# The first turn of two wide attentions: when the late tiles' statistics are taken, and the order of cycle 1's work on three engines

## The chip, the cores and the metric

The kernel runs on one core of a Trainium2 chip. The metric is the device time in microseconds; lower is better.

## The reference

The whole program is eight stages on x (8 batches of 256 tokens by 128) with a context of 8 x 512 x 96. Before each stage x is normalised over its 128 features, and each stage's result is added to x. Two of the stages, the third and the fourth cross attention, are the wide attentions that the change touches. Cut to what matters, with 8 heads of 64 in the one and 16 heads of 64 in the other:

```python
z = layernorm(x)
q, k, v = z @ Wq, ctx @ Wk, ctx @ Wv            # split in heads of 64
sim  = einsum('bihd,bjhd->bhij', q, k) * 64 ** -0.5
attn = softmax(sim)
x = x + einsum('bhij,bjhd->bihd', attn, v).reshape(...) @ Wo + bo
```

## The kernel before, in words

`wide_attention` (line 1945) builds both stages: `l2_attention` (names l2a, 8 heads) and `l3_attention` (names l3a, 16 heads). A **turn** is one of the 8 batches, a **cycle** (c) one pair of heads, so a turn has 4 cycles in l2a and 8 in l3a. In a cycle there are 4 units u: two tiles of 128 queries for two heads, each 128 x 512 scores. Turn 0 is written out by itself (`is_first`), the others run in a loop. Nothing is planned at run time: each engine has its instructions in the order in which the functions below write them, and waits on semaphores.

The way of one cycle: TensorE makes the scores (line 2095) in two halves; VectorE takes the negated maximum of each half (`maxima`, line 2337); ScalarE takes the exponentials of the four units with their sums (`exps`, line 2251); VectorE inverts two sums at a time (`invert`, line 2343); GpSimd multiplies the probabilities by them (line 2039); TensorE turns the four units over (`turned`, line 2108), and VectorE copies units 0 and 2 (`keep_turned`, line 2349), ScalarE units 1 and 3 (line 2258) out of PSUM. This turning over is done one cycle later than the scores, and `weighted` (line 2119: probabilities by values) two cycles later; VectorE's `keep_o` (line 2354) takes its result out of the bank `work[0]`. Queries and keys for the cycle two ahead are projected in between (`project_q` lines 2055 to 2057, `project_k` lines 2068 to 2070, `project_v` lines 2081 to 2083); ScalarE keeps the high part (`keep_q` line 2234, `keep_k` line 2240, `keep_v` line 2244), VectorE the low part (`q_low` line 2327, `k_low` line 2332).

The waits that bear on the change: `turned` of unit 2 waits until VectorE has copied unit 0 out of the same bank, and that of unit 3 for ScalarE's copy of unit 1. `project_v` waits for the `k_low` before it. `weighted` waits for the next `q_low`, and `project_q` for `keep_o`, since they share a bank. `project_k` waits for the `keep_v` before it.

**The late tiles.** Four tiles of 128 tokens are normalised only inside turn 0 of each wide attention, by a class `Ahead` (line 305): `statistics` on VectorE (line 334 four times, line 338 four times, and line 340, which adds epsilon to the variance), the power -1/2 on GpSimd (`gpsimd`, line 345), `apply` on VectorE (line 350 four times) at the end of cycle 2, the turning over on TensorE (line 370) in cycle 3, and its high and low part by ScalarE and VectorE (`keep` line 375, `low` line 379). TensorE turns over cycle 2's unit 0 only when `low` is done (`late.z_lo_ready`). Before the change `statistics` stands in cycle 2 behind both `maxima` and ahead of `keep_o`, and the power between units 1 and 2 of cycle 2 on GpSimd.

Of the kernel before, what the change touches and what calls it, by code (L numbers as in the profile page):

```python
# [1944 lines left out]
def wide_attention(nc, g, name, HEADS, wq, wk, wv, wo, bo, last_tiles, last_tokens, norm_all):  # L1945
# [9 lines left out]
    with ExitStack() as scope:  # L1955
# [16 lines left out]
        ahead = Ahead(s, g, TPB)  # L1972
        late = Ahead(s, g, len(last_tiles), "late")
        late_x = [g.x[:, i, :] for i in last_tiles]
# [20 lines left out]
        def is_first(b):  # L1995
            return isinstance(b, int) and b == 0
# [18 lines left out]
        @block.gpsimd  # L2015
        def _(e):
            def split_ctx(b, side):
                high, low = c_hi[side % SIDES], c_lo[side % SIDES]
                wait(e, m.c_lo_ready, b)
                e.tensor_copy(cT[:, :], g.ctxT[0:DC, bass.ds(b * S, S)]).then_inc(m.c_taken, 1)  # L2020
                e.wait_ge(m.c_taken, b)
                wait(e, m.k_projected, C * (b + 1 - SIDES))
                e.tensor_tensor(high[:, :], cT[:, :], bcast(g.ones[0:DC, 0:1], [DC, S]), ALU.mult).then_inc(m.c_hi_ready, 1)
                e.wait_ge(m.c_hi_ready, b + 1)
                e.tensor_tensor(low[:, :], cT[:, :], high[:, :], ALU.subtract).then_inc(m.c_lo_ready, 1)

            def turn(b, side, more):
                xs = g.x[:, bass.ds(TPB * b, TPB), :]
                e.tensor_tensor(xs, xs, bcast(bo[:, :].unsqueeze(1), [P, TPB, D]), ALU.add).then_inc(m.x_biased, 1)
                for c in range(C):  # L2030
                    for u in range(UNITS):
                        if u == 2 and c == 2:
                            late.gpsimd(e, 0) if is_first(b) else ahead.gpsimd(e, b - 1)
                        if u == 2 and c == C - 3 and more and SIDES == 1:
                            split_ctx(b + 1, 1 - side)
                        if u % 2 == 0:
                            e.wait_ge(m.rinv_ready, 2 * (C * b + c) + u // 2 + 1)
                        n = slot(c, u)
                        e.tensor_tensor(prob[n][:, :], prob[n][:, :], bcast(rinv[:, n:n + 1], [P, S]),  # L2039
                                        ALU.mult).then_inc(m.prob_ready, 1)  # L2040
                    if c == C - 4 and more and SIDES == 2:
                        split_ctx(b + 1, 1 - side)

            turns(e, turn)
            if norm_all:
                ahead.gpsimd(e, B - 1)
# [181 lines left out]
        @block.scalar  # L2228
        def _(e):
            def keep_q(b, c):  # L2230
                n = C * b + c
                e.wait_ge(m.q_projected, n + 1)
                wait(e, m.scores_ready, 2 * (n - 1))
                e.activation(q_hi[c % 2][:, :], work[0][:, 0:T], ACT.Copy, scale=SCALE).then_inc(m.q_hi_ready, 1)

            def keep_k(b, c):
                n = C * b + c
                e.wait_ge(m.k_projected, n + 1)
                wait(e, m.scores_ready, 2 * (n - 1))
                e.activation(k_hi[c % 2][:, :], work[1][:, :], ACT.Copy).then_inc(m.k_hi_ready, 1)  # L2240

            def keep_v(b, c, side, src=work[1]):
                e.wait_ge(m.v_projected, C * b + c + 1)
                e.activation(values_of(side)[:, c % KT, c // KT * 512:(c // KT + 1) * 512], src[:, :], ACT.Copy).then_inc(m.v_kept, 1)

            def exps(b, c, u):
                n, at = C * b + c, slot(c, u)
                if u % 2 == 0:
                    e.wait_ge(m.max_ready, 2 * n + u // 2 + 1)
                wait(e, m.turned, UNITS * (n - 2) + u + 1)  # L2250
                e.activation(prob[at][:, :], bank(u), ACT.Exp, bias=nmax[:, at:at + 1],  # L2251
                             accum_out=rsum[:, at:at + 1]).then_inc(m.exp_ready, 1)

            def keep_turned(b, c, u):
                n = C * b + c
                e.wait_ge(m.turned, UNITS * n + u + 1)
                wait(e, m.o_ready, n - 1)
                e.activation(pT[c % 2][:, :, u % 2, u // 2 * P:u // 2 * P + P],  # L2258
                             tps[u % 2][:, :].rearrange("p (t q) -> p t q", q=P), ACT.Copy).then_inc(m.pT_kept_act, 1)

            def keep_z(b):
                ahead.keep(e, b, g.zT[:, bass.ds(b * T, T)], tps[0][:, 0:T])

            def turn(b, side, more):
                first = is_first(b)
                for c in range(C):
                    onward = c + AHEAD < C or more
                    on = (b, c + AHEAD, side) if c + AHEAD < C else (b + 1, c + AHEAD - C, 1 - side)
                    turn_c = (b, c - 1) if c >= 1 else (b - 1, C - 1)
                    turns_here = c >= 1 or not first  # L2270
                    if c == 0 and first:
                        keep_q(0, 1)
                        exps(b, c, 0)
                        keep_k(0, 1)
                        exps(b, c, 1)
                        exps(b, c, 2)
                        keep_v(0, 0, 0, tps[0])
                        exps(b, c, 3)
                        keep_v(0, 1, 0, tps[1])
                        continue  # L2280
                    if c == 1 and first:
                        keep_v(0, 2, 0)
                        exps(b, c, 0)
                        keep_q(0, 2)
                        exps(b, c, 1)
                        keep_turned(0, 0, 1)
                        keep_k(0, 2)
                        exps(b, c, 2)
                        exps(b, c, 3)
                        keep_turned(0, 0, 3)  # L2290
                        keep_q(0, 3)
                        keep_v(0, 3, 0)
                        continue
                    if c == 2 and first:
                        keep_k(0, 3)
                    exps(b, c, 0)
                    exps(b, c, 1)
                    if c == 3 and first:
                        late.keep(e, 0, last_tokens(g.z_hi), late_rows())
                    if c == 3 and not first:  # L2300
                        keep_z(b - 1)
                    exps(b, c, 2)
                    if onward:
                        keep_v(*on)
                    exps(b, c, 3)
                    if turns_here:
                        keep_turned(*turn_c, 1)
                    if onward:
                        keep_q(*on[0:2])
                        keep_k(*on[0:2])  # L2310
                    if turns_here:
                        keep_turned(*turn_c, 3)

            e.activation(c_hi[0][:, :], g.ctxT[0:DC, 0:S], ACT.Copy).then_inc(m.c_hi_ready, 1)
            keep_q(0, 0)
            keep_k(0, 0)
            turns(e, turn)
            keep_turned(B - 1, C - 1, 1)
            keep_turned(B - 1, C - 1, 3)
            if norm_all:  # L2320
                keep_z(B - 1)

        @block.vector
        def _(e):
            def q_low(b, c):
                e.wait_ge(m.q_hi_ready, C * b + c + 1)
                e.scalar_tensor_tensor(out=q_lo[c % 2][:, :], in0=work[0][:, 0:T], scalar=SCALE, in1=q_hi[c % 2][:, :],
                                       op0=ALU.mult, op1=ALU.subtract).then_inc(m.q_lo_ready, 1)
# [37 lines left out]
            def turn(b, side, more):  # L2366
                first = is_first(b)
                for c in range(C):
# [13 lines left out]
                        continue  # L2382
                    if c == 1 and first:
                        maxima(b, c, 0)
                        q_low(0, 2)
                        maxima(b, c, 1)
                        keep_turned(0, 0, 0)
                        invert(b, c, 0)
                        k_low(0, 2)
                        keep_turned(0, 0, 2)  # L2390
                        invert(b, c, 1)
                        q_low(0, 3)
                        continue
                    maxima(b, c, 0)
# [6 lines left out]
                        ahead_statistics(b - 1)  # L2401
                    if c == 3 and first:
                        late.low(e, 0, last_tokens(g.z_lo), late_rows(), last_tokens(g.z_hi))
                    if c == 2 and first:
                        late.statistics(e, 0, late_x)
                    if c >= 2 or not first:
                        keep_o(*back)
                    if not joins:
# [1585 lines left out]
```

## Time and profile before

| | us |
|---|---|
| median of three runs | 1566.05 |
| lowest and highest run | 1565.95, 1566.26 |
| the profiled execution's own time | 1566.04 |
| its span, first to last instruction | 1563.1 |

Busy shares over the span: TensorE 88%, VectorE 65%, ScalarE 61%, GpSimd 44%. The profiled execution stands 2.9 us above its span, and 0.01 us from the median, so that a difference in its trace can be read as one in the time. l2_attention runs from about 600 to 873 us of the span and l3_attention from about 1009 to 1526. Turn 0 of the one has its first scores at 605.4, that of the other at 1014.2. The timeline lists the instructions of an engine in order: start, duration, engine, line, operation, what it writes and reads, and in brackets how long the engine sat idle before and who ended that. Instructions of one engine overlap a little, so the step from one start to the next is the cost, not the duration. A row that says x4 holds four instructions.

### The profile page before, as it was taken

Reading aid. Unit: us, or ns where it says so; the run is one execution under the profiler, and the core shown is the slowest. Engines: PE = TensorE matmul, PEld = TensorE weight load, DVE = VectorE, ACT = ScalarE, POOL = GpSimd, SP = SyncE. Lnnn points to the kernel's source line nnn. Section 1 sums busy time; section 2 is a strip of 40 time slices with the busy share of each in tenths; the row PEclk is TensorE's granted clock in tenths of the full one; section 3 lists DMA queues with packets and bytes.
Section 4 is the critical chain, followed back from the end, with each engine's and each line's share of the span. In section 5 each row is a group of like instructions: output and inputs, shape, how many; then the busy total and the mean of one; then the engine's idle time right before and its main releaser. Section 6 shows DMA issues by size and latency. Waiting matters only on the chain. (4 is left out here: it accounts for less than half of the span.)

```text
span 1563.1 us, 29903 instructions
## 1 busy us (share of the span) xinstructions
PE 1372.4 (88%) x9545; PEld 1002.0 (64%) x9545; DVE 1013.2 (65%) x2430; ACT 952.1 (61%) x1950; POOL 690.6 (44%) x723
## 2 busy tenths in 40 slices
PE   3799987996887297999999989889999999999996
PEld 2455546985554185677776567657777777777765
DVE  3677864766665835777777456467667677676661
ACT  1578874775565454666666345467667667676652
POOL 2355552110000143556665437446556466565541
PEclk8799997998999597999999989899999999999997
DMA  3400000000000220000000000000000000000002
GB/s 124 111 1 0 0 1 28 1 1 1 1 0 1 78 81 1 1 2 0 0 0 1 1 1 1 1 1 1 2 0 0 0 0 0 0 0 0 1 2 81
DMA packets 29770, 20.51 MB, mean 13 GB/s; under 512 B 9489, under 2 KB 26744, under 8 KB 29688
## 3 DMA queue, kind: packets, MB, share of 16 engines
q1 hardware_dynamic: 28536, 18.95, 4.3%
q8 instruction: 44, 0.72, 0.2%
q10 hardware_dynamic: 1152, 0.52, 0.1%
q14 instruction: 38, 0.31, 0.1%
HBM read 18.42 MB, written 1.05 MB: 12 GB/s over the span
## 5 line engine op out<-in xcount | busy, mean ns | idle before, releaser
L2039 POOL TENSOR_TENSOR l3a_prob<-l3a_prob,l3a_rinv 128x512 f32<-128x512 f32 x256 | 258.9, 1040 | 206.1 <-DVE l3a_rinv L2343 205.7
L2251 ACT ACTIVATE l3a_prob<-l3a_scores_ps,l3a_nmax 128x512 f32<-128x512 f32 x256 | 174.7, 685 | 117.5 <-DVE l3a_nmax L2337 117.5
L2039 POOL TENSOR_TENSOR l2a_prob<-l2a_prob,l2a_rinv 128x512 f32<-128x512 f32 x128 | 129.4, 1040 | 103.1 <-DVE l2a_rinv L2343 102.3
L2337 DVE TENSOR_REDUCE l3a_nmax<-l3a_scores_ps 128x2 f32<-128x1024 f32 x128 | 155.8, 1218 | 22.2 <-PE l3a_scores_ps L2095 22.2
L897 ACT ACTIVATE l0a_prob<-l0a_scores_ps,l0a_k_scale 128x1024 f32<-128x1024 f32 x128 | 135.4, 1112 | 40.4 <-PE l0a_scores_ps L793 39.9
L2108 PE MATMUL l3a_turned_ps<-const,l3a_prob 128*128 128x128 f32 x1024 | 145.8, 276 | 4.1 <-DVE l3a_probT L2349 2.5
L2349 DVE COPY l3a_probT<-l3a_turned_ps 128x512 f32<-128x512 f32 x128 | 88.4, 691 | 83.5 <-PE l3a_turned_ps L2108 83.4
L2108 PEld LDWEIGHTS l3a_turned_ps<-const,l3a_prob 128*128 128x128 f32 x1024 | 120.7, 142 | 27.3 <-issue 11.0
L2119 PE MATMUL l3a_work_ps<-l3a_probT,l3a_v 128*64 128x256 f32 x1024 | 124.6, 385 | 2.7 <-DVE x_tokens L2364 1.7
L2251 ACT ACTIVATE l2a_prob<-l2a_scores_ps,l2a_nmax 128x512 f32<-128x512 f32 x128 | 87.4, 685 | 56.7 <-DVE l2a_nmax L2337 56.7
L2119 PEld LDWEIGHTS l3a_work_ps<-l3a_probT,l3a_v 128*64 128x64 f32 x1024 | 69.4, 136 | 52.2 <-issue 24.1
L2258 ACT ACTIVATE l3a_probT<-l3a_turned_ps 128x512 f32<-128x512 f32 x128 | 77.0, 601 | 33.0 <-PE l3a_turned_ps L2108 29.7
L2337 DVE TENSOR_REDUCE l2a_nmax<-l2a_scores_ps 128x2 f32<-128x1024 f32 x64 | 77.8, 1217 | 9.7 <-PE l2a_scores_ps L2095 9.7
L290 POOL TENSOR_TENSOR l1f_front_all_rstd<-l1f_front_all_var_eps,neg_half 128x8 f32<-128x8 f32 x4 | 6.6, 1653 | 163.2 <-DVE l1f_front_all_var_eps L262 163.2
L2108 PE MATMUL l2a_turned_ps<-const,l2a_prob 128*128 128x128 f32 x512 | 74.1, 279 | 3.1 <-DVE l2a_probT L2349 1.5
L2349 DVE COPY l2a_probT<-l2a_turned_ps 128x512 f32<-128x512 f32 x64 | 44.2, 691 | 44.6 <-PE l2a_turned_ps L2108 44.6
L2108 PEld LDWEIGHTS l2a_turned_ps<-const,l2a_prob 128*128 128x128 f32 x512 | 60.6, 144 | 16.6 <-issue 9.9
L807 PE MATMUL l0a_pv_ps<-l0a_prob,l0a_v 128*32 128x256 f32 x1024 | 69.4, 389 | 0.0
L2119 PE MATMUL l2a_work_ps<-l2a_probT,l2a_v 128*64 128x256 f32 x512 | 62.3, 385 | 4.4 <-DVE x_tokens L2364 3.3
L1348 PEld LDWEIGHTS l0f_y_ps<-w_l_w,l0f_hidden 128*128 128x128 f32 x512 | 61.4, 192 | 1.9
L1348 PE MATMUL l0f_y_ps<-w_l_w,l0f_hidden 128*128 128x128 f32 x512 | 62.4, 275 | 0.0
L2095 PE MATMUL l3a_scores_ps<-l3a_k_hi,l3a_q_hi 64*128 64x512 f32 x256 | 57.7, 447 | 1.5 <-DVE l3a_k_lo L2332 0.6
(672 smaller groups left out, 3587.5 us busy)
## 6 DMA issues: line engine op xcount, KB each, us to landing
l1f_w<-in_L_ffn_w SPq DMA_DIRECT2D x16, 256.0 KB, 2.7
load_ctx_rows<-in_ctx SPq DMA_DIRECT2D x1, 1536.0 KB, 7.5
l3f_experts_w<-in_L_ffn_W SPq DMA_DIRECT2D x24, 64.0 KB, 1.9
w_l_w<-in_L_ffn_W SPq DMA_DIRECT2D x1, 1024.0 KB
out_x<-x_tokens SPq DMA_DIRECT2D x8, 128.0 KB, 1.9
const<-in_constants SPq DMA_DIRECT2D x1, 589.0 KB
w_l_wo<-in_L_xattn_Wo SPq DMA_DIRECT2D x1, 512.0 KB
l0f_raw_f<-in_L_xattn_W_f SPq DMA_DIRECT2D x1, 512.0 KB, 4.5
```

Of the source, the lines that this page charges most:

```text
L290: e.tensor_tensor(self.rstd[:, tiles], self.var[:, tiles], self.g.neg_half[:, tiles], ALU.pow).then_inc(self.rstd_ready, 1)
L807: last = e.matmul(pvps[grp % 2][32 * j:32 * j + 32, 0:T], v[:, t, GH * grp + j, :], prob[n % 4][:, j * T:(j + 1) * T], start=t == 0, stop= ...
L897: e.activation(prob[n % 4][:, :], sc[n % 2][:, :], ACT.Exp, scale=kscale[:, n % KT:n % KT + 1]).then_inc(m.prob_ready, 1)
L1348: last = e.matmul(yps[n % 2][:, tokens], h[n % 3][:, f, tokens], g.l0_w2[:, x, f, :], start=f == 0, stop=f == FT - 1)
L2039: e.tensor_tensor(prob[n][:, :], prob[n][:, :], bcast(rinv[:, n:n + 1], [P, S]), ALU.mult).then_inc(m.prob_ready, 1)
L2095: last = e.matmul(bank(2 * i + h), q[c % 2][rows, queries], key[c % 2][rows, :], start=k == 0, stop=k == 2, tile_position=(HD * h, 0))
L2108: last = e.transpose(tps[u % 2][:, t * P:(t + 1) * P], prob[slot(c, u)][:, t * P:(t + 1) * P], g.ident)
L2119: last = e.matmul(work[0][HD * h:HD * h + HD, 0:T], values_of(side)[:, t, head], pT[c % 2][:, t, h, :], start=t == 0, stop=t == KT - 1, ti ...
L2251: e.activation(prob[at][:, :], bank(u), ACT.Exp, bias=nmax[:, at:at + 1], accum_out=rsum[:, at:at + 1]).then_inc(m.exp_ready, 1)
L2258: e.activation(pT[c % 2][:, :, u % 2, u // 2 * P:u // 2 * P + P], tps[u % 2][:, :].rearrange("p (t q) -> p t q", q=P), ACT.Copy).then_inc( ...
L2337: e.tensor_reduce(nmax[:, at:at + 2], sps[:, i * 1024:(i + 1) * 1024].rearrange("p (h k) -> p h k", h=2), AX.X, ALU.max, negate=True).then ...
L2349: e.tensor_copy(pT[c % 2][:, :, u % 2, u // 2 * P:u // 2 * P + P], tps[u % 2][:, :].rearrange("p (t q) -> p t q", q=P)).then_inc(m.pT_kept ...
```

## The change

`late.statistics` moves from cycle 2 to the end of cycle 1 on VectorE, ahead of the last `q_low`. The power on GpSimd moves from the middle to the top of cycle 2 in turn 0; the other turns keep theirs. In cycle 1 of turn 0 VectorE takes the second `maxima` and the copy of unit 0 ahead of `q_low(0, 2)`, and ScalarE takes the first exponential ahead of `keep_v(0, 2)`. The number of instructions and what they compute are the same.

```diff
@@ gpsimd turn
                 for c in range(C):
                     for u in range(UNITS):
-                        if u == 2 and c == 2:
-                            late.gpsimd(e, 0) if is_first(b) else ahead.gpsimd(e, b - 1)
+                        if u == 0 and c == 2 and is_first(b):
+                            late.gpsimd(e, 0)
+                        if u == 2 and c == 2 and not is_first(b):
+                            ahead.gpsimd(e, b - 1)
@@ scalar turn
                     if c == 1 and first:
+                        exps(b, c, 0)
                         keep_v(0, 2, 0)
-                        exps(b, c, 0)
                         keep_q(0, 2)
@@ vector turn
                     if c == 1 and first:
                         maxima(b, c, 0)
-                        q_low(0, 2)
                         maxima(b, c, 1)
                         keep_turned(0, 0, 0)
+                        q_low(0, 2)
                         invert(b, c, 0)
                         k_low(0, 2)
                         keep_turned(0, 0, 2)
                         invert(b, c, 1)
+                        late.statistics(e, 0, late_x)
                         q_low(0, 3)
                         continue
@@
-                    if c == 2 and first:
-                        late.statistics(e, 0, late_x)
```

## Rows read from the trace of the kernel before

**Rows 1.** Windows: us, busy PE PEld DVE ACT POOL, PEclk, DMA, GB/s; l3_attention from cycle 4.
```profile
1052.00:1520.00 468.00, 463.86 (x3448) 345.34 (x3446) 325.94 (x617) 315.82 (x783) 272.22 (x275) 1.00 0.00 0
```

**Rows 2.** Timeline of VectorE, l3_attention, cycles 1 to 3: start, duration, line.
```profile
1021.14 1.20 DVE L2337 TENSOR_REDUCE l3a_nmax<-l3a_scores_ps 128x2 f32<-128x1024 f32 x1
...
1024.88 1.21 DVE L2337 TENSOR_REDUCE l3a_nmax<-l3a_scores_ps 128x2 f32<-128x1024 f32 x1
1026.01 0.68 DVE L2349 COPY l3a_probT<-l3a_turned_ps 128x512 f32<-128x512 f32 x1
...
1028.84 0.42 DVE L2327 SCALAR_TENSOR_TENSOR l3a_q_lo<-l3a_work_ps,l3a_q_hi 128x256 fp32r<-128x256 f32 x1 [0.58 <-ACT l3a_q_hi L2234]
1029.89 1.22 DVE L2337 TENSOR_REDUCE l3a_nmax<-l3a_scores_ps 128x2 f32<-128x1024 f32 x1 [0.62 <-PE l3a_scores_ps L2095]
...
1033.84 0.86 DVE L334 BATCH_NORM_STATS2 l3a_late_stats<-x_tokens 128x6 f32<-128x128 f32 x4
...
1035.24 0.42 DVE L2354 COPY l3a_oT<-l3a_work_ps 128x256 f32<-128x256 f32 x1
...
1038.94 2.48 DVE L350 TENSOR_SCALAR l3a_late_z<-x_tokens,l3a_late_mean_var,l3a_late_rstd 128x128 f32<-128x128 f32 x4
1041.34 1.21 DVE L2337 TENSOR_REDUCE l3a_nmax<-l3a_scores_ps 128x2 f32<-128x1024 f32 x1
...
1044.56 0.69 DVE L379 TENSOR_TENSOR z_lo<-l3a_turned_ps,z_hi 128x512 fp32r<-128x512 f32 x1 [0.27 <-ACT z_hi L375]
```

**Rows 3.** Timeline of TensorE, l3_attention, cycles 1 to 4.
```profile
1026.84 1.06 PE L2108 MATMUL l3a_turned_ps<-const,l3a_prob 128*128 128x128 f32 x8 [1.98 <-DVE l3a_probT L2349]
...
1028.10 0.40 PE L2081 MATMUL l3a_work_ps<-l_wv_hi,l3a_c_hi 96*128 96x512 f32 x1
...
1031.37 1.95 PE L2119 MATMUL l3a_work_ps<-l3a_probT,l3a_v 128*64 128x256 f32 x16
...
1045.39 0.63 PE L2108 MATMUL l3a_turned_ps<-const,l3a_prob 128*128 128x128 f32 x4 [1.21 <-DVE z_lo L379]
...
1049.93 0.49 PE L2095 MATMUL l3a_scores_ps<-l3a_k_hi,l3a_q_hi 64*128 64x512 f32 x2
...
1054.19 0.60 PE L2108 MATMUL l3a_turned_ps<-const,l3a_prob 128*128 128x128 f32 x4
...
1057.09 0.50 PE L2095 MATMUL l3a_scores_ps<-l3a_k_hi,l3a_q_hi 64*128 64x512 f32 x2
```

**Rows 4.** Timeline of ScalarE, l3_attention, cycle 1.
```profile
1022.97 0.60 ACT L2244 ACTIVATE l3a_v<-l3a_work_ps 128x512 f32<-128x512 f32 x1 [1.45 <-PE l3a_work_ps L2083]
1023.46 0.68 ACT L2251 ACTIVATE l3a_prob<-l3a_scores_ps,l3a_nmax 128x512 f32<-128x512 f32 x1
```

**Rows 5.** Timeline of GpSimd, l3_attention, cycle 2.
```profile
1038.79 2.04 POOL L2039 TENSOR_TENSOR l3a_prob<-l3a_prob,l3a_rinv 128x512 f32<-128x512 f32 x2
```

**Rows 6.** Line 340 by tile: min/median/max ns.
```profile
L340 DVE TENSOR_SCALAR l2a_ahead_var_eps<-l2a_ahead_mean_var x7: 802/811/912, 663.7 to 854.2; 128x2 f32<-128x2 f32 x7
```

**Rows 7.** Line 350 by tile: min/median/max ns.
```profile
L350 DVE TENSOR_SCALAR l3a_late_z<-x_tokens,l3a_late_mean_var,l3a_late_rstd x4: 336/654/1077, 1038.9 to 1041.1; 128x128 f32<-128x128 f32 x4
```

**Rows 8.** Timeline of VectorE, l2_attention, cycles 1 to 3.
```profile
623.87 1.23 DVE L2337 TENSOR_REDUCE l2a_nmax<-l2a_scores_ps 128x2 f32<-128x1024 f32 x1 [0.63 <-PE l2a_scores_ps L2095]
...
635.33 1.21 DVE L2337 TENSOR_REDUCE l2a_nmax<-l2a_scores_ps 128x2 f32<-128x1024 f32 x1
```

**Rows 9.** Timeline of TensorE, l2_attention, cycle 3.
```profile
639.37 0.63 PE L2108 MATMUL l2a_turned_ps<-const,l2a_prob 128*128 128x128 f32 x4 [1.22 <-DVE z_lo L379]
```

**Rows 10.** Windows around the two falls of TensorE's clock, and one without.
```profile
636.50:639.90 3.40, 1.49 (x8) 1.04 (x9) 2.86 (x6) 3.33 (x9) 0.19 (x1) 1.00 0.00 0
639.90:643.40 3.50, 3.50 (x16) 3.10 (x16) 0.76 (x2) 1.90 (x5) 3.50 (x4) 0.51 0.00 0
1025.60:1029.00 3.40, 2.16 (x16) 1.79 (x18) 2.67 (x7) 2.85 (x9) 2.16 (x3) 1.00 0.00 0
1042.70:1046.10 3.40, 1.68 (x10) 1.22 (x10) 2.72 (x6) 3.40 (x9) 0.37 (x1) 1.00 0.00 0
```

## Prediction

> **What bounds the kernel now.** The windows come first: from cycle 4 to the end of l3_attention TensorE is busy 463.86 of 468 us at the full clock [rows 1]. So a wide attention has no slack once it runs, and what is saved before that is kept to the end. The share of busy time says nothing about turn 0; there the timelines of the four engines, laid side by side, do. In cycle 1 TensorE sits idle 1.98 us until VectorE has copied unit 0 of cycle 0, and in cycle 3 it sits 1.21 us until VectorE has the late tiles' low part [rows 3]. Before both, VectorE is late with work that it could have done: its copy at 1026.01 stands behind a `maxima` at 1024.88, and `keep_o` at 1035.24 behind 1.40 us of statistics that began at 1033.84 [rows 2]. Both stages do the same, so I walk through l3_attention and then give l2_attention's differences. I place each instruction at the latest of three: its engine is free, what it waits for is done, what stands before it has been issued. The steps from one start to the next are those of the rows: 1.13 us for a `maxima` (1024.88 to 1026.01), 0.60 for a copy of 128x512 on VectorE, 0.34 for a `q_low`, 0.33 for a `keep_o`, 0.66 for an exponential with its sum.
>
> **Cycle 1, new order, l3.** `maxima` ends its first half at 1021.14 + 1.20 = 1022.34 [rows 2]. ScalarE's first exponential began only at 1023.46, behind `keep_v` at 1022.97 [rows 4]; it moves to 1022.38. `keep_v` then starts at 1023.04, 0.07 later; its waiter, `project_k`, comes at 1023.92, so that costs nothing. VectorE's second `maxima` goes from 1024.88 to 1022.27, the copy of unit 0 from 1026.01 to 1023.40, when TensorE has turned it, and `q_low` behind it stands at 1024.17, 0.37 earlier than it was. TensorE's idle 1.98 us are gone. The next thing that is late is `k_low`: ScalarE's `keep_k` now stands behind the exponentials and ends at 1025.79, `k_low` ends at 1026.50, and `project_v` starts at 1026.61 where it was 1028.10 [rows 3]: **1.49 us**, not 1.98.
>
> **Statistics moved, l3.** They start behind the second `invert` at 1027.23. They cost 1.40 where GpSimd is idle. Now GpSimd is multiplying cycle 1's probabilities beside them, 1027.40 to 1029.44. The rows of the other turns show what that does: line 340, ahead of its two-element add, took 802 to 912 ns in l2's seven [rows 6], until GpSimd's multiply was over. I put its end at 1029.48, so statistics cost 2.17 here. `q_low` behind them goes from 1028.84 to 1029.40, 0.56 later [rows 2]. Its waiter is `weighted`, which went at 1031.37 [rows 3] and could now go at 1029.88; q_low ends at 1029.82, so it is just covered, and if the cover fails each us late is a us of TensorE. Behind it `maxima` of cycle 2 goes from 1029.89 to 1029.74. In cycle 2 the 1.40 us are gone: `keep_o` goes from 1035.24 to 1032.60, 2.64 earlier. The power at the top of cycle 2 lies on GpSimd from 1029.56 to 1030.57; the first multiply of cycle 2 comes at 1033.16, so it is hidden with 2.6 us to spare, and the bound is 1 us if it is not. TensorE's `project_k` follows `keep_v` at 1034.09, the scores of cycle 3 at 1035.87, both some 2.5 earlier.
>
> **Apply, l3.** The four instructions of line 350 took 2.40 us from start to start (1038.94 to 1041.34 [rows 2]), though the shortest took 336 ns [rows 7]; the long ones ended as each of GpSimd's two multiplies did [rows 5]. They lay there because the power stood between units 1 and 2. With it moved, GpSimd's units 2 and 3 run 1035.20 to 1037.24 and apply starts at 1036.45, in the last of them: 0.79 for the first, 0.25 for each of three, 1.54 us. The bounds are 1.0 (no collision) and 2.40 (both again). The next `maxima` goes from 1041.34 to 1037.99: 3.35 earlier. The Trainium skill, page "SBUF — State Buffer", section "Who interferes with whom", calls the port pair of VectorE and GpSimd an exclusive lock, which a GpSimd instruction or a VectorE copy or tensor_scalar in a two-port mode holds for its whole length, the second to issue waiting. By that rule line 340 must slow down where it is now put, which speaks against the change, and apply must speed up; without it the sum would be 0.8 us less in each stage, and the trace agrees with it in rows 6 and 7. `low` then goes from 1044.56 to 1041.19, and TensorE's turning over, which waits for it, from 1045.39 to 1042.02: **3.37 us** [rows 2, 3].
>
> **The clock, l3.** Just after 1046 the granted clock falls to its lower level, 1.2 GHz, for some 3.4 us; before it fell TensorE had been busy 1.68 of 3.40 us. It fell likewise in l2 at 639.9, after 1.49 of 3.40, and not after 2.16 of 3.40 in cycle 1 [rows 10]. From turning over to the next scores it took 4.54 us at the low level (1045.39 to 1049.93) and 2.90 a cycle on (1054.19 to 1057.09) [rows 3]. In the changed kernel the wait of 0.75 us for `k_low` in cycle 3 falls into `weighted` and goes, and the 1.21 us for `low` stay, so around them TensorE is busy some 2.2 of each 3.40 us, as in the stretch after which it did not fall. I take the fall as gone: 1.64, together **5.01 us**.
>
> **l2_attention.** The same walk. Cycle 1 gains less, since TensorE is itself the slow one there, at the low clock for most of it: `project_v` goes only 0.68 earlier. The statistics meet GpSimd's last multiply and push `maxima` of cycle 2 from 623.87 to 624.52 [rows 8], 0.65 later, covered because `keep_o` gains 1.84 behind it. `maxima` of cycle 3 goes from 635.33 to 632.79 [rows 8], and TensorE's turning over from 639.37 to 636.82 [rows 9], **2.55 us**; with the fall at 639.9 gone, by the same 1.63, **4.18 us**.
>
> **The sum.** 1566.04 - 5.01 - 4.18 = 1556.85, and the profiled execution stands at the median, so **1556.9 us**. The waits name no DMA in either stage, and [rows 1] leave nothing that could take the gain back.
>
> **The rivals.** (1) The clock falls all the same, in both stages. For it: the wait for `low` of 1.2 us remains, and it is again followed by sparse work. Then the gain is 3.37 + 2.55 = 5.92: 1560.1 us; 18%. In one stage alone: 1558.5; 16%. (2) Less than that is gained: line 350 meets two multiplies again and `q_low` is a us late for `weighted`; each stage then loses 0.9 + 1, and with the falls kept 1562.3; 6%. (3) The gain is taken back: turn 0's TensorE waits move to another engine, GpSimd or ScalarE, and cycle 4 comes when it did. Against it are the 463.86 of 468 us. 1566; 9%. (4) Slower: turn 0's TensorE gets new sparse stretches, and the clock falls after them or its low level lasts longer at the starts and ends of the stages. One such fall costs 1.64; with the 5.92 gained it decides from the fourth on, and with six the time is 1566.04 - 5.92 + 9.84 = 1570.0; 3%. Nothing in the rows has that many waits.
>
> **How the numbers follow.** The forecast has 48%. A measurement of this kernel can tell about 0.2%, 3.1 us. Faster by more than that: 48 + 18 + 16 + 6 = 88%; within it 9%; slower 3%. The range reaches down by one fall less at a stage's border, 1556.9 - 1.6 = 1555.3, and up to rival 1 with 0.9 for an apply that meets both multiplies in one stage, 1561.0. Left out are rivals 2 to 4, 18%.
>
> **What would show it.** In l3: no idle of TensorE before unit 2's turning over in cycle 1, the copy of unit 0 some 2.6 us earlier; line 340 for the late tiles at 0.8 to 0.9 us in place of 0.17; line 350's four at about 1.5 us; `low` 3.4 us earlier against the first scores; a granted clock of 1.00 through cycles 2 to 4 in both stages. If the clock window still reads 0.5 behind `low`, rival 1 holds. I am wrong if `keep_o` of cycle 0 is earlier by 2.6 us and the scores of cycle 4 are not, or if a wait of TensorE for `q_low` appears ahead of `weighted`.

## The result, and the profile after

The changed kernel takes 1556.49 us (median of six runs, 1554.84 to 1557.52), the kernel before 1566.38 beside it; the ratio is 0.9936, with a 95% interval of 0.9923 to 0.9949. The profiled execution took 1556.84, which is 9.20 us under that of the kernel before. The prediction was 1556.9, and 9.19 under.

The time can be followed to its places with one ruler that I use for all runs. **D** is the time from the first `maxima` of turn 0 to the first scores of cycle 4, once in each stage. Before, it is 643.90 - 606.58 = 37.32 us in l2 and 1049.93 - 1015.75 = 34.18 in l3 (the end in l3 is in [rows 3]; the other three are from the timelines of VectorE and TensorE of the kernel before):

```profile
606.58 1.22 DVE L2337 TENSOR_REDUCE l2a_nmax<-l2a_scores_ps 128x2 f32<-128x1024 f32 x1 [1.90 <-PE l2a_scores_ps L2095]
...
643.90 0.50 PE L2095 MATMUL l2a_scores_ps<-l2a_k_hi,l2a_q_hi 64*128 64x512 f32 x2
...
1015.75 1.23 DVE L2337 TENSOR_REDUCE l3a_nmax<-l3a_scores_ps 128x2 f32<-128x1024 f32 x1 [2.25 <-PE l3a_scores_ps L2095]
```

Next, VectorE in l3 after the change (timeline: start, duration, engine, line, operation; lines behind 2039 have moved by two); they answer to [rows 2]:

```profile
1011.96 1.23 DVE L2339 TENSOR_REDUCE l3a_nmax<-l3a_scores_ps 128x2 f32<-128x1024 f32 x1 [1.14 <-PE l3a_scores_ps L2097]
...
1019.64 0.69 DVE L2351 COPY l3a_probT<-l3a_turned_ps 128x512 f32<-128x512 f32 x1
...
1022.06 0.69 DVE L2334 TENSOR_TENSOR l3a_k_lo<-l3a_work_ps,l3a_k_hi 128x512 fp32r<-128x512 f32 x1 [0.81 <-ACT l3a_k_hi L2242]
...
1023.48 0.85 DVE L334 BATCH_NORM_STATS2 l3a_late_stats<-x_tokens 128x6 f32<-128x128 f32 x4
...
1024.78 0.93 DVE L340 TENSOR_SCALAR l3a_late_var_eps<-l3a_late_mean_var 128x4 f32<-128x4 f32 x1
1025.62 0.41 DVE L2329 SCALAR_TENSOR_TENSOR l3a_q_lo<-l3a_work_ps,l3a_q_hi 128x256 fp32r<-128x256 f32 x1
1025.95 1.21 DVE L2339 TENSOR_REDUCE l3a_nmax<-l3a_scores_ps 128x2 f32<-128x1024 f32 x1
...
1028.81 0.41 DVE L2356 COPY l3a_oT<-l3a_work_ps 128x256 f32<-128x256 f32 x1
...
1032.62 1.64 DVE L350 TENSOR_SCALAR l3a_late_z<-x_tokens,l3a_late_mean_var,l3a_late_rstd 128x128 f32<-128x128 f32 x4
1034.18 1.21 DVE L2339 TENSOR_REDUCE l3a_nmax<-l3a_scores_ps 128x2 f32<-128x1024 f32 x1
...
1037.40 0.69 DVE L379 TENSOR_TENSOR z_lo<-l3a_turned_ps,z_hi 128x512 fp32r<-128x512 f32 x1 [0.28 <-ACT z_hi L375]
```

Read them against the first row as zero. The copy of unit 0 comes at 7.68, where it was at 10.26. The statistics now stand ahead of `q_low`, line 340 takes 0.93 us, and cycle 2's `maxima` (13.99) is 0.15 earlier than before (14.14). `keep_o` comes at 16.85, where it was 19.49, and `low` at 25.44, where it was 28.81: 2.64 and 3.37 us, to the hundredth what the prediction had.

TensorE's timeline in l3, and then in l2 with the first row of VectorE's ahead of it, answers to [rows 3] and [rows 9]:

```profile
1022.81 0.50 PE L2083 MATMUL l3a_work_ps<-l_wv_hi,l3a_c_hi 96*128 96x512 f32 x1
...
1026.17 1.95 PE L2121 MATMUL l3a_work_ps<-l3a_probT,l3a_v 128*64 128x256 f32 x16
...
1038.24 0.63 PE L2110 MATMUL l3a_turned_ps<-const,l3a_prob 128*128 128x128 f32 x4 [1.22 <-DVE z_lo L379]
...
1041.16 0.50 PE L2097 MATMUL l3a_scores_ps<-l3a_k_hi,l3a_q_hi 64*128 64x512 f32 x2
```

```profile
607.92 1.23 DVE L2339 TENSOR_REDUCE l2a_nmax<-l2a_scores_ps 128x2 f32<-128x1024 f32 x1 [1.86 <-PE l2a_scores_ps L2097]
...
638.09 0.63 PE L2110 MATMUL l2a_turned_ps<-const,l2a_prob 128*128 128x128 f32 x4 [1.23 <-DVE z_lo L379]
...
641.01 0.50 PE L2097 MATMUL l2a_scores_ps<-l2a_k_hi,l2a_q_hi 64*128 64x512 f32 x2
```

D is 1041.16 - 1011.96 = 29.20 in l3 and 641.01 - 607.92 = 33.09 in l2: 4.98 and 4.23 us less, where 5.01 and 4.18 were forecast. Of TensorE's two waits in front of cycle 3's turning over only that of 1.22 us (1.23 in l2) for `low` is left; the one of 0.75 us for `k_low` is gone. From the turning over to the scores it takes 2.92 us in both stages, not 4.54. The two lines by tile show the meeting with GpSimd, which the prediction had drawn from [rows 6, 7] (min/median/max ns):

```profile
L340 DVE TENSOR_SCALAR l3a_late_var_eps<-l3a_late_mean_var x1: 925/925/925, 1024.8 to 1024.8; 128x4 f32<-128x4 f32 x1
```
```profile
L350 DVE TENSOR_SCALAR l3a_late_z<-x_tokens,l3a_late_mean_var,l3a_late_rstd x4: 332/334/874, 1032.6 to 1033.9; 128x128 f32<-128x128 f32 x4
```

Only one of line 350's four is long now. And the windows (stretch, length, busy PE, PEld, DVE, ACT, POOL, granted clock) answer to [rows 1] and [rows 10]:

```profile
633.50:636.90 3.40, 3.36 (x25) 1.96 (x23) 3.40 (x6) 1.62 (x5) 0.00 (x0) 1.00 0.00 0
636.90:640.30 3.40, 2.21 (x17) 2.07 (x18) 1.93 (x6) 2.90 (x8) 1.88 (x2) 1.00 0.00 0
1034.70:1038.10 3.40, 2.33 (x17) 1.20 (x12) 3.12 (x5) 2.67 (x8) 0.00 (x0) 1.00 0.00 0
1038.10:1041.50 3.40, 3.26 (x24) 2.91 (x26) 1.83 (x6) 2.70 (x7) 2.92 (x3) 1.00 0.00 0
1043.00:1511.00 468.00, 464.11 (x3448) 345.48 (x3444) 326.42 (x617) 316.52 (x783) 272.34 (x275) 1.00 0.00 0
```

The clock is 1.00 where it fell before, and the rest of l3 is as full of TensorE's work as it was (464.11 of 468 us, 463.86 before). What is left of the 9.20 us is outside: l2 began 1.34 later in this execution, the way from cycle 4 of l2 to l3 took 0.90 less, the way from there to the end 0.37 more, and the time outside the span 0.80 less. These four come to 0.01 together, by luck: nothing in them is changed, and they move by as much between executions of kernels that are the same up to there.

### The profile page after: what moved, and what is told of

It reads as the page before. It is cut to its first block and busy times, and to the rows that moved or that the text cites. A ratio compares the mean times of both kernels' runs of the same rounds, so it can differ in the third digit from the quotient of the medians.

```text
span 1554.7 us, 29892 instructions
## 1 busy us (share of the span) xinstructions
PE 1368.7 (88%) x9534; PEld 999.9 (64%) x9545; DVE 1013.7 (65%) x2430; ACT 954.0 (61%) x1950; POOL 691.5 (44%) x723
```

## The experiments

All runs in one table, each ratio against runs of the kernel before taken beside it (their medians were 1566.38, 1565.49 and 1566.80 us); "falls" says whether the clock went down to its lower level behind `low`, in l2 and in l3. Where it says single run, the time is rough: the kernel before alone ran from 1563.3 to 1568.8 us beside them, the changed one from 1554.0 to 1560.1.

| run | D l2 / l3 | falls | us | ratio to before (95%) |
|---|---|---|---|---|
| before | 37.32 / 34.18 | yes / yes | 1566.38 | |
| changed | 33.09 / 29.20 | no / no | 1556.49 | 0.9936 (0.9923 to 0.9949) |
| power back | 33.86 / 31.48 | no / yes | 1559.50 | 0.9962 (0.9948 to 0.9976) |
| order alone | 35.08 / 32.76 | no / yes | 1560.02 | 0.9966 (0.9955 to 0.9978) |
| statistics alone | 33.58 / 32.03 | no / no | 1558.94 | 0.9958 (0.9943 to 0.9972) |
| before, idle products in the wait | 35.69 / 32.60 | no / no | 1561.78 | 0.9977 (0.9968 to 0.9987) |
| changed again | 33.09 / 29.17 | no / no | 1556.31 | 0.9939 (0.9925 to 0.9953) |
| high part early | 32.71 / 28.80 | no / no | 1552.79 | single run |
| epsilon on GpSimd | 32.96 / 29.03 | no / no | 1558.16 | single run |
| both of these | 32.14 / 28.68 | no / no | 1553.97 | 0.9919 (0.9906 to 0.9931) |
| before again | 37.32 / 34.18 | yes / yes | 1565.89 | single run |
| before, shifted by five | 35.70 / 32.57 | no / no | 1567.17 | single run |
| before, shifted by two | 37.31 / 35.78 | yes / yes | 1565.48 | single run |
| changed, shifted by five | 32.67 / 29.19 | no / no | 1559.21 | single run |

**1. The power back in its old place.**

```diff
-                        if u == 0 and c == 2 and is_first(b):
-                            late.gpsimd(e, 0)
-                        if u == 2 and c == 2 and not is_first(b):
-                            ahead.gpsimd(e, b - 1)
+                        if u == 2 and c == 2:
+                            late.gpsimd(e, 0) if is_first(b) else ahead.gpsimd(e, b - 1)
```

> The changed kernel with the power on GpSimd put back between units 1 and 2 of cycle 2; all else stays. Measure D: from the first maxima of a stage's turn 0 to the first scores of cycle 4; l2 / l3 before 37.32 / 34.18, changed 33.09 / 29.20 us. Theory (the power's place makes line 350 meet two multiplies of GpSimd): line 350's four take 2.1 to 2.4 us in place of 1.56, so low is 0.6 to 0.8 us later in each stage: D 33.8 / 30.0 with the clock at its full level. The wait of TensorE for k_low in cycle 3 comes back too, and with it perhaps the clock's fall, 1.6 more in each: D 35.5 / 31.6. In all 1.5 to 4.8 us over the changed kernel. Rival (the place of the power does nothing, since GpSimd has 2.6 us to spare): D and time as in the changed kernel.

Line 350's four took 2.37 and 2.36 us from the first start to the last end, where they took 1.64 in the changed kernel; `low` came 0.77 and 0.71 later. l2 stayed at that (D 33.86). In l3 the clock fell too, and D is 2.28 over the changed kernel. TensorE's timeline of l3 in this run:

```profile
1037.81 0.50 PE L2081 MATMUL l3a_work_ps<-l_wv_hi,l3a_c_hi 96*128 96x512 f32 x1 [0.60 <-DVE l3a_k_lo L2332]
...
1040.00 1.08 PE L2108 MATMUL l3a_turned_ps<-const,l3a_prob 128*128 128x128 f32 x4 [1.22 <-DVE z_lo L379]
...
1044.49 0.50 PE L2095 MATMUL l3a_scores_ps<-l3a_k_hi,l3a_q_hi 64*128 64x512 f32 x2
```

The wait for `k_low`, here 0.60 us, is back beside the one for `low`, the transposes behind it take 1.08 in place of 0.63, and the scores come 4.49 us after them. The rival falls: GpSimd had time to spare, but VectorE had not.

**2. Cycle 1's new order alone.**

```diff
+                        exps(b, c, 0)
                         keep_v(0, 2, 0)
-                        exps(b, c, 0)
...
-                        q_low(0, 2)
                         maxima(b, c, 1)
                         keep_turned(0, 0, 0)
+                        q_low(0, 2)
```

> The kernel before with the new order of cycle 1 alone (VectorE's second maxima and copy of unit 0 ahead of q_low, ScalarE's exponential ahead of keep_v). Theory: l3 gains 1.49, l2 0.68 us, and nothing more, as statistics and line 350 cost what they cost: D 36.6 / 32.7, time 2.2 under the kernel before. The falls of the clock behind low stay, for TensorE still waits for k_low and for low there; if they go, 1.6 less each. Rival (the order alone makes the whole gain): D near 33 / 29.

`low` is 0.65 earlier in l2 and 1.40 in l3, near the 0.68 and 1.49 of the walk. In l3 D follows (32.76). In l2 it is 35.08, 1.6 lower still, because the clock did not fall: though TensorE had both waits, 0.76 us for `k_low` and 1.23 for `low`, as long as before. In the 3.40 us that end half a us behind the start of the turning over, TensorE was busy 1.49 us, as in the kernel before [rows 10], and the granted clock stayed at 1.00 behind them. That was the first sign that the fall doesn't hang on the waits alone. The rival, that the order alone makes the whole gain, is out. Which part of the order does it, VectorE's or ScalarE's, was not taken apart.

**3. The statistics and the power moved alone.**

```diff
                         invert(b, c, 1)
+                        late.statistics(e, 0, late_x)
                         q_low(0, 3)
...
-                    if c == 2 and first:
-                        late.statistics(e, 0, late_x)
```

(and the power at the top of cycle 2 as in the change)

> The kernel before with the statistics moved to the end of cycle 1 and the power to the top of cycle 2, cycle 1's order as it was. Theory: q_low ahead of weighted comes about 1.0 us later and is just covered; keep_o of cycle 0 is 1.40 earlier, line 350 0.8 shorter, low 2.2 earlier in each stage: 4.5 in all, D 35.1 / 31.9; with both falls of the clock gone too, as I expect, 7.7 in all, D 33.5 / 30.3. Rival (q_low is not covered and TensorE waits for it ahead of weighted): D less than 1 us under the kernel before, and weighted in its idle column waits for q_lo.

l2 is as expected: `low` 2.14 earlier, no fall, D 33.58. l3 missed by 1.7: `low` was only 0.54 earlier. TensorE's timeline shows why:

```profile
1022.55 1.79 PE L2110 MATMUL l3a_turned_ps<-const,l3a_prob 128*128 128x128 f32 x8 [1.98 <-DVE l3a_probT L2351]
...
1024.78 0.63 PE L2083 MATMUL l3a_work_ps<-l_wv_hi,l3a_c_hi 96*128 96x512 f32 x1
1025.21 0.63 PE L2084 MATMUL l3a_work_ps<-l_wv_lo,l3a_c_hi 96*128 96x512 f32 x1
```

The clock fell in cycle 1, behind the wait of 1.98 us for the copy of unit 0, which the new order of cycle 1 removes. The windows read 0.50 there, the low level, and the products of `project_v` take 0.63 us in place of the 0.39 to 0.50 of the changed kernel:

```profile
1024.00:1026.00 2.00, 2.00 (x8) 1.44 (x6) 1.92 (x13) 0.98 (x2) 2.00 (x3) 0.50 0.00 0
```

The kernel before has the same wait of 1.98 us there and no fall behind it. `weighted` came 17.21 us after the first `maxima`, 1.59 later than before. Not `q_low` but the clock made it late, so the rival is not borne out either. This run also tells what sets line 340's length. VectorE's timeline and then GpSimd's, both in l3:

```profile
1025.51 0.17 DVE L340 TENSOR_SCALAR l3a_late_var_eps<-l3a_late_mean_var 128x4 f32<-128x4 f32 x1
```
```profile
1022.55 4.03 POOL L2041 TENSOR_TENSOR l3a_prob<-l3a_prob,l3a_rinv 128x512 f32<-128x512 f32 x4 [3.10 <-DVE l3a_rinv L2345]
```

GpSimd's four multiplies follow one another at 1.01 us, so the third ends near 1025.6, 0.1 us after line 340 began at 1025.51: it took 0.17 us. In l2 of this run 0.36 us of a multiply were left when it began, and it took 0.42; in the changed kernel's l3, at 1024.78, 0.90 were left of the one that ends at 1025.68, and it took 0.93. So in these three cases, as the prediction had read [rows 6], the instruction ends when the multiply that it meets does, some 0.03 to 0.07 us behind it. It does not wait for the next one, though that follows at once: in l3 it was over at 1025.68, when the fourth multiply had only begun.

**4. The clock's share by itself.** In the kernel before, four idle products of 128x512 in TensorE's wait for `low`.

```diff
+                    if c == 3 and first:
+                        e.wait_ge(m.pT_kept_act, 2 * (n - 1))
+                        keep_warm(4)
                     if turns_here:
                         turned(*turn_c, 0)
```

> The kernel before with four idle matrix products of 128x512 added on TensorE in cycle 3 of turn 0, where it waits for low; nothing reads them. Theory (the fall of the clock follows TensorE's sparse work there and costs 1.63 us a stage by itself): the granted clock reads 1.00 from cycle 2 to 4 in both stages, turning over to scores takes 2.9 in place of 4.5 us: D 35.7 / 32.5, time 3.3 under the kernel before. Rival A (the slow stretch is hidden beside other engines): the clock stays full but D stays 37.3 / 34.2. Rival B (the fall does not depend on this wait): the clock falls as before, D as before.

D fell by 1.63 and 1.58 us, and the time by 0.23% (3.2 by D, 2.0 to 5.0 by the interval). `low` stands where it stood (31.92 and 28.83). From TensorE's timeline of l2:

```profile
639.57 0.63 PE L2108 MATMUL l2a_turned_ps<-const,l2a_prob 128*128 128x128 f32 x4 [0.30 <-DVE z_lo L379]
...
642.50 0.50 PE L2095 MATMUL l2a_scores_ps<-l2a_k_hi,l2a_q_hi 64*128 64x512 f32 x2
```

2.93 us to the scores, with nothing else changed. The slow stretch was not hidden, and both rivals are out: the prediction's term of 1.63 is right. That it adds to what is gained in front of it shows against this run, which has no fall either: the changed kernel's D is lower than here by 2.60 us in l2 and 3.40 in l3, 6.0 in all.

**5. The changed kernel again, and two small edits.** The high part of the late tiles behind the first exponential in place of the second; epsilon added on GpSimd, ahead of the power; and both.

```diff
                     exps(b, c, 0)
-                    exps(b, c, 1)
                     if c == 3 and first:
                         late.keep(e, 0, last_tokens(g.z_hi), late_rows())
+                    exps(b, c, 1)
```

```diff
+                            late.add_eps(e, 0)        # line 340's instruction, on GpSimd
                             late.gpsimd(e, 0)
```

> The changed kernel once more, to compare the next ones on the same chip. D (first maxima of turn 0 to the first scores of cycle 4; changed kernel 33.09 / 29.20 in l2 / l3) within 0.1 of that if the clock stays full behind low as it did; 1.6 more in a stage in which it falls. Rival (the changed kernel's full clock was luck of one execution): a fall in at least one of the stages.

> The changed kernel with the high part of the late tiles taken by ScalarE behind the first exponential of cycle 3 in place of the second. Theory: low no longer waits 0.35 us for it, nothing else is late, D 32.74 / 28.85. Rival: the second exponential, 0.5 us later, makes ScalarE's copies of units 1 and 3 late and TensorE waits there: D unchanged.

> The changed kernel with epsilon added by GpSimd ahead of the power instead of by VectorE alone. Theory (line 340's 0.93 us are spent beside work that VectorE waits for anyway): keep_o of cycle 0 0.2 us earlier, D 32.9 / 29.0. Rival (they are on the path): D 32.2 / 28.3.

> The changed kernel with the high part behind the first exponential, and with epsilon added by GpSimd ahead of the power instead of by VectorE (line 340), so that VectorE meets no multiply there. Theory: VectorE's 0.93 us go, q_low ahead of weighted and the maxima of cycle 2 come 0.8 us earlier; but the second maxima waits for k_low, which waits for ScalarE, so keep_o gains only 0.2 us; with the 0.35 of the other edit D 32.55 / 28.67, some 1.1 us in all, hard to see in the time. Rival (line 340's wait is on the path): D 0.9 lower for it, 31.8 / 27.9.

The changed kernel gives the same D to 0.03 us, without a fall. The early high part takes 0.38 and 0.37 off that; TensorE's wait for `low` goes from 1.22 to 0.86, as its timeline in l3 has it:

```profile
1033.30 0.63 PE L2110 MATMUL l3a_turned_ps<-const,l3a_prob 128*128 128x128 f32 x4 [0.86 <-DVE z_lo L379]
```

The rival, that ScalarE's copies come late, is out. Epsilon on GpSimd takes 0.13 and 0.14, not 0.9. In l3 the first `maxima` of cycle 2 comes 0.98 us earlier (12.99 against 13.97 from the stage's first), the second only 0.15 (15.55 against 15.70): line 340's wait was on VectorE's queue and hardly on the path. GpSimd does both in the time that it had to spare:

```profile
1027.10 0.23 POOL L345 TENSOR_SCALAR l3a_late_var_eps<-l3a_late_mean_var 128x4 f32<-128x4 f32 x1
1027.41 1.04 POOL L350 TENSOR_TENSOR l3a_late_rstd<-l3a_late_var_eps,neg_half 128x4 f32<-128x4 f32 x1
```

Both edits together have the lowest median (1553.97) of the kernels that were run more than once, 0.81% under the kernel before. But the intervals of this ratio and of the changed kernel's (0.9906 to 0.9931, 0.9925 to 0.9953) overlap; by D they are worth 0.49 in l3 and 0.95 in l2, of which some 0.4 is cycle 1's slow stretch lying better (`keep_o` 20.15 us after the first `maxima` in place of 20.75; in the shifted changed kernel below it is 20.32, and D 0.42 lower). It beats the kernel before; that it beats the changed one is shown by D and not by the time.

**6. Does the order of the work decide on the fall, or its place in time?**

```diff
             project_k(0, 0, 0)
-            keep_warm(5)
+            keep_warm(10)        # 7 in the run shifted by two
```

> The kernel before once more, one look. Theory (the clock's fall behind low depends on where in time the sparse stretch lies, not on the order alone, as the run with the new order alone kept both of TensorE's waits in l2 and had no fall): D 37.3 or 35.7 in l2, 34.2 or 32.5 in l3, from one execution to the next. Rival (the order alone decides): D 37.32 / 34.18 again, falls in both.

> The kernel before with five more idle matrix products ahead of turn 0's first scores in both stages, 1.2 to 2.2 us; what follows is the same. D counts from the first maxima, so it holds only what comes after. Theory (place in time decides on the fall): D as before or 1.6 less, not the same choice in both stages as in the other run of the kernel before. Rival (the order decides): D 37.32 / 34.18 with falls in both, time 2.5 to 4.5 us over the kernel before.

> The kernel before with two more idle products ahead of turn 0's first scores. Theory (place in time decides where both waits are there): D 37.3 or 35.7 in l2, 34.2 or 32.5 in l3, nothing between. Rival (adding products ahead of the scores keeps the clock up by itself): D 35.7 / 32.5 as with five.

> The changed kernel with the same five more idle products ahead of turn 0's first scores in both stages as in the shifted kernel before. Theory (the changed kernel no longer has the wait for k_low in cycle 3, and without it the clock does not fall wherever the stretch lies): D 33.1 / 29.2, clock full from cycle 2 to 4. Rival (the changed kernel has no fall only because its stretch came to lie well in time): a fall in at least one stage, D 1.6 more there.

The kernel before again gave its 37.32 and 34.18 with both falls, as the rival of that run had it (its theory allowed it too); its first `maxima` in l2 stood at 606.45, and at 606.58 in the first profile, so the place in time had hardly moved. With five products more it stood at 610.45. TensorE's timeline of l2 in the kernel before again, and in the same kernel shifted by five products:

```profile
637.06 0.50 PE L2081 MATMUL l2a_work_ps<-l_wv_hi,l2a_c_hi 96*128 96x512 f32 x1 [0.75 <-DVE l2a_k_lo L2332]
...
639.25 0.63 PE L2108 MATMUL l2a_turned_ps<-const,l2a_prob 128*128 128x128 f32 x4 [1.23 <-DVE z_lo L379]
...
643.77 0.50 PE L2095 MATMUL l2a_scores_ps<-l2a_k_hi,l2a_q_hi 64*128 64x512 f32 x2
```

```profile
641.04 0.50 PE L2081 MATMUL l2a_work_ps<-l_wv_hi,l2a_c_hi 96*128 96x512 f32 x1 [0.75 <-DVE l2a_k_lo L2332]
...
643.23 0.63 PE L2108 MATMUL l2a_turned_ps<-const,l2a_prob 128*128 128x128 f32 x4 [1.22 <-DVE z_lo L379]
...
646.15 0.50 PE L2095 MATMUL l2a_scores_ps<-l2a_k_hi,l2a_q_hi 64*128 64x512 f32 x2
```

The two waits are alike to 0.01 us, 0.75 and 1.22 or 1.23; the scores follow 4.52 us after the one and 2.92 after the other. The windows over these stretches, again first and shifted second, show TensorE equally busy in front (2.02 and 2.03 of 4 us) and then the low level in the first alone:

```profile
636.00:638.00 2.00, 1.25 (x6) 0.56 (x4) 2.00 (x3) 1.56 (x5) 0.00 (x0) 1.00 0.00 0
638.00:640.00 2.00, 0.77 (x7) 0.78 (x7) 1.31 (x5) 2.00 (x6) 0.42 (x1) 0.95 0.00 0
640.00:642.00 2.00, 2.00 (x10) 1.81 (x9) 0.68 (x2) 0.85 (x4) 2.00 (x3) 0.50 0.00 0
```
```profile
640.00:642.00 2.00, 1.25 (x6) 0.54 (x4) 2.00 (x3) 1.57 (x5) 0.00 (x0) 1.00 0.00 0
642.00:644.00 2.00, 0.78 (x8) 0.80 (x8) 1.32 (x5) 2.00 (x6) 0.43 (x1) 1.00 0.00 0
644.00:646.00 2.00, 2.00 (x17) 1.81 (x16) 0.83 (x3) 1.49 (x5) 2.00 (x3) 1.00 0.00 0
```

With two products more in place of five both stages fell again, and l3 fell in cycle 1 as well (`weighted` 17.24, D 35.78). I had expected nothing between 34.2 and 32.5 and nothing over it, and missed that second place. The changed kernel, shifted by five, kept the full clock in both stages. Counted over the profiles in which TensorE waited for `k_low` ahead of `low` (before twice, power back, order alone, and before shifted twice: 12 passes of turn 0), 8 had the fall; where that wait was gone (the changed kernel three times, statistics alone, and the three runs of the small edits: 14 passes), none had the fall behind `low`.

So the fall behind `low` came only where the order leaves TensorE both waits, and with both waits there something else decides. No run speaks against the place in time. It isn't the five products by themselves, since the order alone parted in the same way (no fall in l2, one in l3) with no product added. But which place brings the fall is open, and no run takes away or puts back the wait for `k_low` and nothing else: that this wait makes the difference rests on the count.

## Why the prediction was right

**Cycle 1.** `project_v` gained 1.49 us in the walk. It starts at 10.85 from the first `maxima` (12.35 before): 1.50. In l2 it gained 0.75, forecast 0.68. `k_low` was the next thing late, as forecast: VectorE waits 0.81 us for ScalarE's `keep_k` ahead of it, it ends at 1022.75 and `project_v` starts at 1022.81. The order alone gave 1.40 and 0.65 at `low`.

**Statistics.** Forecast 2.17 us from the first to the `q_low` behind them, measured 1025.62 - 1023.48 = 2.14, with line 340 at 0.93. The cover of `weighted` held: it started 1.41 earlier (14.21 against 15.62), with no wait for `q_low` shown. In l2 cycle 2's `maxima` came 0.59 later, forecast 0.65. The epsilon on GpSimd puts the price of the meeting at 0.13 to 0.14 us, so rival 2 had little under it from this side. Its time was also added up wrong: 5.92 less 1.9 in each stage leaves 2.1 us, so with the falls kept it is 1563.9; 1562.3 is the time with one of them gone. At 1563.9 it lies within 3.1 us of the kernel before, and the chance of "faster by more than that" is 82%, not 88%.

**Apply.** Forecast 1.54 from start to start, measured 1034.18 - 1032.62 = 1.56. `low` was 3.37 earlier in l3, as forecast; the turning over was 2.62 earlier in l2, forecast 2.55. The power's old place costs 0.71 to 0.77 at `low`, and it also brings TensorE's wait for `k_low` back, which the prediction named only as going.

**The clock.** Forecast 1.64 and 1.63; by the idle products 1.58 and 1.63. No fall stayed in the six passes of the changed order, nor in the six of its three small edits, so the 34% for that look high. TensorE was busy 2.21 and 2.33 of 3.40 us around the wait for `low`, where some 2.2 was forecast. But the reason given was short: I argued from this busy share alone, and took the falls as belonging to the kernel before. They don't always: the same kernel, moved by five products, has neither, and its share in front is the same. Its two falls came up in both profiles of it, so the forecast that takes them as the state before was right for this pair of kernels, and 3.2 of the 9.2 us is a gain over where the kernel before happened to lie. Nothing in the argument showed that the kernel before would have its falls in the runs to come, so for this part the agreement owes something to luck. The timed runs point the same way as the two profiles: the interval of the ratio is 8.0 to 12.1 us, and without the falls only 6.0 would be gained. These 6.0 are gained ahead of the fall and don't hang on it.

**Sum.** Over `low` 3.37 + 2.63, over the clock 1.61 + 1.60, together 9.21. The parts don't add: the order alone brought 1.40 + 0.65 at `low`, the statistics alone 2.14 in l2, where together they brought 2.63 and not 2.79. The 0.16 is near the price of the meeting with the multiply (line 340 took 0.92 us there and 0.42 with the statistics alone), but no run shows that it is the same. **Rivals 3 and 4** are out: from cycle 4 on l3 keeps what it has, and the only new fall seen, in l3's cycle 1, came in two runs with the old order of cycle 1 and its wait of 1.98 us (statistics alone, and before shifted by two). None of the eight profiles with the new order has it.

## What to carry to other kernels

In an order written by hand, place each instruction at the latest of its engine, its inputs and its predecessor, with the steps of the profile: queues that are busy 65% and 61% of the time hid 6 us in the first cycles of two stages, and such a walk found them to a tenth (5.92 forecast, 6.00 measured). Where VectorE and GpSimd both work on SBUF, move a small VectorE instruction by when GpSimd is between two of its own, and ask whether anybody waits for it before paying for that. And before a slow clock is put into a sum as lost or won, shift the whole by different amounts and compare: the kernel before kept its falls with two products more and lost them with five.

## What had not been expected of the hardware

The granted clock's fall, given nearly the same two waits (0.60 to 0.76 and 1.22 us), came in 8 of 12 passes: five products of extra work in front took it away in both stages, two did not and brought a third, in cycle 1. Where in time the waits lay would fit this, but no run shows it to be the cause. It costs 1.6 us each time. The spread from run to run is larger than this: the kernel before ran from 1563.3 to 1568.8 us and the first `maxima` of l2 from 605.1 to 610.7 us after the start in the kernels whose code up to there is the same. The Trainium skill, page "TensorE: Matmul & The Clock Gate", Part 1, calls the rise of the clock at a kernel's start run-variable, since it depends on where the first product lands. The runs here show the like for a fall in the middle of a kernel: 4.52 us against 2.92 for the same piece of work.
